# Decoder block on one core: output product from rounded parts, new order of TensorE's work in the sharing cycles, weight rests on POOL, last block's first products moved into attention

## The chip, the cores and the metric

One core of a Trainium2 chip runs the whole program. The engines are TensorE (PE in the profile, with its weight loads as PEld), VectorE (DVE), ScalarE (ACT), GpSimd (POOL) and SyncE (SP, which issues most of the DMAs). The metric is the device time in microseconds.

## The reference

```python
x = _layernorm(x + attn(x, up_w, gate_w, local_point, local_approx_output, fuse_weight, ...))   # 6 Taylor orders + SwiGLU, F = 1248
x = _layernorm(x + xattn(x, ctx, mask, position_bias, ln_weight, w_q, w_k, w_v, w_out))         # 32 heads of 128, 8 x 128 tokens
x = _layernorm(x + ffn(x, Wg, Wu, Wd, ag, au, ad))                                               # F = 1376, ternary weights

def xattn(h, kv, mask, bias, ln_weight, w_q, w_k, w_v, w_out):      # cut
    x = rmsnorm(h, ln_weight)
    q, k, v = heads(x @ w_q.T), heads(kv @ w_k.T), heads(kv @ w_v.T)
    score = einsum('bqhd,bkhd->bhqk', q, k) + bias
    score = softmax(where(mask, score, -inf));  score = where(mask, score, 0)
    return h + einsum('bhqk,bkhd->bqhd', score, v).reshape(...) @ w_out.T
```

All arrays are float32; x is 8 x 128 x 512. In these inputs the mask leaves at most the last 32 of 128 keys of each sample open, and the kernel has a path ("few") for that case.

## The kernel before

The eight samples are two halves of four (512 columns each). The first block runs for half 0 and half 1 (0 to about 221 us of the profile), cross attention from there to about 613, and the last feed-forward block to the end. float32 products that run in one pass use operands that are rounded on ACT ("hi", an fp32r copy) with the rest on DVE ("lo" = whole - hi, line 1288); hi·hi + hi·lo + lo·hi then makes three matmuls (`passes`, line 543). A plain float32 matmul stands in the profile as two weight loads and two MATMUL records.

Attention is 64 cycles n = 0..63, one per head and half, in four blocks of 16. In blocks 0 and 2 (n = 0..15 and 32..47) the cycle is a *sharing* one: it makes keys and values from rounded parts for both halves and keeps the other half's (`kept_k`, `kept_v`). In blocks 1 and 3 it is a *reading* one, with the kept ones. The names used below:

- `queries(n)` (line 716): 4 matmuls into bank 0, copied by ACT to `t_ring` (1160). Cycle n makes those of n+6.
- `keys(n)` (543, weights `wk_hi`, `wk_lo`): 12 matmuls into bank 1, copied by ACT. Cycle n makes those of n+7, so keys are made in cycles 0..8 and 25..40. `split_k` on ACT (1060) and `rest_k` on DVE (1288) prepare the weights.
- `values(n)` (543, weights in `b_hi`, `b_lo` by `split_v` on ACT, 1069, and `rest_v` on DVE): 12 matmuls into bank 3, copied to `v_sb` (1186).
- `turn(n)` (778): transposes the probabilities into bank 3, which ACT copies to `prob_t` (1167). The same bank holds the values.
- `outer(n)` (824): values times `wo` into bank 1, copied to `u_sb` (1193).
- `weigh(n)` (846): four matmuls of 32 rows each, one for each sample, probabilities times `u_sb`, added up in four accumulators. They use four different row groups of TensorE and run side by side.
- `group_scores` (729 and 751): in the second and third cycle of every four, the scores of the next four heads; `add_mask`, `find_max`, `divide` on DVE (1544, 1550 and 1552, 1558 to 1562) and `exponentials` on ACT (1174) make the softmax.
- `features` and `chunk`: transposes of the normalised rows and their copies, for the queries' second half (part 1) and for the last block (part 2, cycles 62 and 63).

The order is written out by hand for each engine as a loop over n, and every engine works strictly through its own list; semaphores tie them together. In cycle n TensorE's order before is queries(n+6), turn(n-1), weigh(n-2), keys(n+7), values(n), outer(n-1), scores. POOL does the normalisations' scales and rows (lines 445 to 485), two reductions over partitions (499, 509) and nothing in the cycles themselves. After the cycles come the last block's first `gate` and `up` (543, `A30`), and then a branch into the last block. ACT's silu of that first gate needs another table of functions (ACT_TABLE_LOAD).

## Time and profile before

| | us |
|---|---|
| median of 3 runs | 754.17 (753.99 to 755.84) |
| the profiled execution | 753.72 |
| its span | 751.9 |
| DVE busy | 522.2 (69%) |
| ACT busy | 408.6 (54%) |
| POOL busy | 94.8 (13%) |

The span runs from the first instruction to the last; 1.8 us of the execution lie around it. Busy times are sums over an engine's records, and shares are of the span. Matmul records overlap their neighbours, so the distance between the starts of two pieces of work is the better measure of what TensorE spends on one. PEclk is the granted share of TensorE's clock. "Idle" in brackets behind a row is the time in which the engine stood still ahead of it, with what released it ("issue": nothing that the profile shows).

### The profile page before, as it was taken

To read this page: it belongs to the slowest core of one execution; us is meant where nothing else is said; L and a number is where in the kernel's file an instruction comes from. 1 tells how busy PE (TensorE), PEld (TensorE's weight loads), DVE (VectorE), ACT (ScalarE), POOL (GpSimd) and SP (SyncE) were. 2 spreads that over 40 slices of the span, in tenths; PEclk is the share of its full clock that TensorE was granted. 3 is DMA by queue.
4 is the path that set the end of the run, shared out by engine and by line. 5 is a ranking of instruction groups with operands and counts; after the bars stand their busy time and mean duration, and the time that the engine had idled before them with its cause. 6 is when DMAs were issued, how large, how long until landed. Compare 5 with 4: busy or idle time off the path is not lost.

```text
span 751.9 us, 12237 instructions
## 1 busy us (share of the span) xinstructions
PE 716.2 (95%) x4082; PEld 555.7 (74%) x4082; DVE 522.2 (69%) x848; ACT 408.6 (54%) x747; POOL 94.8 (13%) x88
## 2 busy tenths in 40 slices
PE   8999999999999999999999999999999779998993
PEld 6788888888878878776667787877656257886882
DVE  6555687588664875686876678667897828669565
ACT  6333323432355676776776666666676644454552
POOL 2000000074003600000000000000050004105403
PEclk9999999999999999999999999999999999999997
DMA  8455532545556765677997776668785513442631
GB/s 307 152 206 206 179 119 70 163 168 187 183 208 199 251 195 181 216 258 233 306 316 236 240 238 190 192 215 267 263 297 180 169 44 117 135 151 98 204 122 56
DMA packets 70681, 145.10 MB, mean 193 GB/s; under 512 B 7920, under 2 KB 8192, under 8 KB 69984
## 3 DMA queue, kind: packets, MB, share of 16 engines
q1 hardware_dynamic: 69200, 137.26, 55.7%
q0 software_dynamic: 1200, 6.70, 2.3%
q8 instruction: 34, 0.56, 0.3%
q10 hardware_dynamic: 224, 0.39, 0.2%
q14 instruction: 23, 0.19, 0.1%
HBM read 142.23 MB, written 2.10 MB: 192 GB/s over the span
## 4 chain that ended last, share of the span: by engine, by line
PE 86%; DVE 5%; issue 3%; DMA 2%; ACT 2%; POOL 1%; SPq 0%; ACTq 0%; DVEq 0%; POOLq 0%
PE bank L543 38%; PE acc L543 16%; PE acc L846 8%; PE bank L751 7%; PE bank L824 7%; PE bank L716 7%; PE bank L778 1%; PE bank L729 1%; DMA b_raw<-b 1%; DMA a_raw<-a 1%; PE bank L575 1%; DVE tile_lo L1288 1%; ACT v_sb L1186 1%; DVE a_lo L1288 1%; DMA wq<-wqn 1%
## 5 line engine op out<-in xcount | busy, mean ns | idle before, releaser
L543 PE MATMUL bank<-feat_hi,a_hi 128*128 128x512 f32 x348 | 137.7, 396 | 2.2 <-ACT u_sb L1193 0.8
L543 PE MATMUL bank<-feat_lo,a_hi 128*128 128x512 f32 x348 | 136.5, 392 | 2.1 <-issue 2.1
L1288 DVE TENSOR_TENSOR a_lo<-a_raw,a_hi 128x1024 fp32r<-128x1024 f32 (+3 forms) x47 | 56.8, 1208 | 94.5 <-ACT a_hi L1000 86.9
L543 PE MATMUL acc<-b_hi,tile_hi 128*128 128x512 f32 x224 | 87.8, 392 | 4.9 <-DVE tile_lo L1288 3.0
L543 PE MATMUL acc<-b_hi,tile_lo 128*128 128x512 f32 x224 | 87.3, 390 | 0.0
L543 PEld LDWEIGHTS bank<-feat_hi,a_hi 128*128 128x128 f32 x348 | 65.9, 189 | 22.6 <-issue 4.0
L543 PEld LDWEIGHTS bank<-feat_lo,a_hi 128*128 128x128 f32 x348 | 65.9, 189 | 13.5
L846 PE MATMUL acc<-u_sb,prob_t 32*128 32x512 f32 x512 | 73.0, 640 | 0.0
L543 PE MATMUL bank<-feat_hi,a_lo 128*128 128x512 f32 x180 | 70.1, 389 | 0.0
L1017 ACT ACTIVATE tile_hi<-pair 128x512 fp32r<-128x512 f32 x54 | 33.9, 628 | 66.3 <-DVE pair L1350 37.4
L751 PEld LDWEIGHTS bank<-t_ring,xn 128*128 128x128 f32 x512 | 62.1, 192 | 8.5 <-issue 7.2
L445 POOL TENSOR_SCALAR scale<-moments 128x4 f32<-128x4 f32 (+1 forms) x9 | 2.6, 287 | 515.1 <-DVEq L1420 514.8
L1558 DVE TENSOR_REDUCE row_sum<-prob 128x4 f32<-128x512 f32 x64 | 43.7, 683 | 31.9 <-ACT prob L1174 30.5
L1160 ACT ACTIVATE t_ring<-bank 128x512 f32<-128x512 f32 x64 | 38.2, 597 | 46.3 <-PE bank L716 46.0
L751 PE MATMUL bank<-t_ring,xn 128*128 128x128 f32 x512 | 62.3, 275 | 0.0
L1193 ACT ACTIVATE u_sb<-bank 128x512 f32<-128x512 f32 x64 | 38.2, 598 | 28.4 <-PE bank L824 25.8
L543 PEld LDWEIGHTS acc<-b_hi,tile_hi 128*128 128x128 f32 x224 | 42.0, 188 | 15.6 <-DVE b_lo L1288 4.2
L543 PE MATMUL acc<-b_lo,tile_hi 128*128 128x512 f32 x136 | 52.9, 389 | 0.0
L1288 DVE TENSOR_TENSOR b_lo<-b_raw,b_hi 128x512 fp32r<-128x512 f32 x56 | 40.0, 715 | 14.9 <-ACT b_hi L1007 14.6
L1007 ACT ACTIVATE b_hi<-b_raw 128x512 fp32r<-128x512 f32 x56 | 34.8, 623 | 26.8 <-PE acc L543 21.6
L1026 ACT ACTIVATE gated<-bank 128x512 f32<-128x512 f32 x20 | 12.0, 598 | 67.8 <-PE bank L543 67.8
L543 PEld LDWEIGHTS acc<-b_hi,tile_lo 128*128 128x128 f32 x224 | 42.1, 188 | 8.6
(152 smaller groups left out, 1555.8 us busy)
## 6 DMA issues: line engine op xcount, KB each, us to landing
wqi<-ax SPq DMA_DIRECT2D x64, 256.0 KB, 3.3
wq<-wqn SPq DMA_DIRECT2D x64, 256.0 KB, 3.7
wv<-wvh SPq DMA_DIRECT2D x64, 256.0 KB, 4.0
wo<-bx SPq DMA_DIRECT2D x64, 256.0 KB, 4.0
a_raw<-w SPq DMA_DIRECT2D x22, 512.0 KB, 4.1
wk<-ax SPq DMA_DIRECT2D x43, 256.0 KB, 3.8
a_raw<-a SPq DMA_DIRECT2D x21, 512.0 KB, 5.4
b_raw<-b SPq DMA_DIRECT2D x34, 256.0 KB, 2.7
```

Source lines behind the costliest of these rows:

```text
L543: mm = pe.matmul(out_ap, w, x, start=start and k == 0, stop=stop and k == len(products) - 1, skip_group_check=True)
L716: mm = pe.matmul(bank[0][:, c * P:(c + 1) * P], wq[par][:, c * P:(c + 1) * P], few_keys, start=True, stop=True)
L751: mm = pe.matmul(bank[2][:, b * P:(b + 1) * P].rearrange("p (k h) -> p h k", h=GH), xn[half][:, c, b * SEQ:(b + 1) * SEQ], t_ring[g % 2][: ...
L824: mm = pe.matmul(bank[1][:], few_values, wo[slot][:], start=True, stop=True)
L846: mm = pe.matmul(acc[b][:], prob_t[par][rows, 0:P], u_sb[par][rows, :], start=begins, stop=ends, skip_group_check=True)
L1007: act.activation(b_hi[par][:], b_raw[par][:], ACT.Copy).then_inc(b_hi_ok, 1)
L1017: act.activation(tile_hi[par][:], src, ACT.Copy).then_inc(tile_hi_ok, 1)
L1026: act.activation(gated[:], bank[0][:], ACT.Silu).then_inc(silu_ok, 1)
L1160: act.activation(t_ring[n // GH % 2][:, n % GH].rearrange("p c b k -> p (c b k)"), bank[0][:], ACT.Copy).then_inc(t_ok, 1)
L1193: act.activation(u_sb[n % 2][:], bank[1][:], ACT.Copy).then_inc(u_ok, 1)
L1288: return dve.tensor_tensor(out_ap, whole, high, ALU.subtract)
L1558: dve.tensor_reduce(row_sum[:], prob[n % 2][:], AX_X, ALU.add).then_inc(sum_ok, 1)
```

## The change

Four things are changed in the attention path and one at its end.

1. In sharing cycles the output product of `weigh` is made of rounded parts: ACT writes `u_hi` in place of `u_sb` and also `p_hi` (128x128) from `prob_t`, DVE writes `p_lo` and `u_lo` (the latter from bank 1 and `u_hi`), and TensorE does 12 matmuls of 32 rows in fp32r in place of 4 in float32. Whoever writes bank 1 next waits for `u_lo_ok` as well.
2. TensorE's order in a sharing cycle becomes keys(n+7) between the two halves of queries(n+6), then turn, outer, values.
3. The rests of the key and value weights go to POOL, from the weights of n = 9 (keys) and n = 2 (values) on; DVE keeps the first ones. POOL's new loop stands behind its second reduction over partitions.
4. In reading cycles `values` (there only a mark) stands ahead of `weigh`, and ACT copies the values ahead of `copy_outer`.
5. The four transposes for the last block move to cycles 54, 57, 58 and 59, its first gate to cycle 60 and its first up to cycle 61 (into bank 2), its silu on ACT to cycle 62, and the loads that they need are issued at n = 50 and n = 58. The features of the last block have tiles of their own (`last_hi`, `last_lo`).

```diff
@@ POOL
             pool.tensor_copy(low_flag[:], piece_all[:, 1:2]).then_inc(flag_ok, 1)
+            for n in range(POOL_V - 1, HN):
+                k = n + LEAD_K + 1
+                if k < HN and shared(k):
+                    pool.wait_ge(wk_hi_ok, shared_count(k))
+                    pool.tensor_tensor(wk_lo[k % 2], wk[k % WK_RING][:], wk_hi[k % 2].bitcast(F32),
+                                       ALU.subtract).then_inc(wk_rest_ok, 1)
+                if n + 1 < HN and shared(n + 1):
+                    pool.wait_ge(wv_hi_ok, shared_count(n + 1))
+                    pool.tensor_tensor(wv_lo[(n + 1) % 2], wv[(n + 1) % 2][:], wv_hi[(n + 1) % 2].bitcast(F32),
+                                       ALU.subtract).then_inc(wv_rest_ok, 1)
             normalise(2)
@@ TensorE, keys
-                        pe.wait_ge(wk_lo_ok, shared_count(n))
+                        if n < POOL_K:                     # POOL_K = LEAD_K + 2 = 9
+                            pe.wait_ge(wk_lo_ok, n + 1)
+                        else:
+                            pe.wait_ge(wk_rest_ok, shared_count(n) - POOL_K)
@@ TensorE, weigh
+                    if few and shared(n):
+                        for k, (weights, values_) in enumerate(((p_hi, u_hi), (p_hi, u_lo), (p_lo, u_hi))):
+                            for b in range(HB):
...
+                                mm = pe.matmul(acc[b][:], weights[par][rows, :], values_[par][rows, :], start=begins and k == 0,
+                                               stop=ends and k == 2, skip_group_check=True)
@@ TensorE, the cycles
+                    if making:
                         keys(n + LEAD_K)
+                        if n >= 2:
+                            weigh(n - 2)
+                        if few:
+                            queries(n + LEAD_T, range(C // 2, C))
+                        if n >= 1:
+                            turn(n - 1)
+                            outer(n - 1)
...
+                        values(n)
...
                     if late:
+                        if n + LEAD_K < HN:
+                            keys(n + LEAD_K)
+                        turn(n - 1)
+                        if few:
+                            values(n)
+                        weigh(n - 2)
+                        if n in FEATURES_2:                # 54, 57, 58, 59
+                            features(2, FEATURES_2[n], resid[:, TT:2 * TT, :], min(n + LEAD_T + 1, HN))
...
                         outer(n - 1)
...
+                    if n == GATE_30:                       # 60
+                        pe.wait_ge(feat_lo_ok, C)
+                        gate(A30, A30 % 2, 0, HALVES * F1, last=True)
+                    if few and n == UP_30:                 # 61
+                        pe.wait_ge(added_ok, HN)
+                        up(A30 % 2, 0, HALVES * F1, last=True, into=bank[2])
@@ ACT
                 act.activation(prob_t[n % 2][:], bank[3][:], ACT.Copy).then_inc(turned_ok, 1)
+                if shared(n):
+                    act.wait_ge(turned_ok, n + 1)
+                    act.activation(p_hi[n % 2][:], prob_t[n % 2][:, 0:P], ACT.Copy).then_inc(p_hi_ok, 1)
...
+                if n == HN - 2:
+                    silu(A30, HALVES * F1, True, 0)
@@ DVE
+            def rest_p(n):
+                dve.wait_ge(p_hi_ok, shared_count(n))
+                low(p_lo[n % 2][:], prob_t[n % 2][:, 0:P], p_hi[n % 2][:].bitcast(F32)).then_inc(p_lo_ok, 1)
+            def rest_u(n):
+                dve.wait_ge(u_ok, n + 1)
+                low(u_lo[n % 2][:], bank[1][:], u_hi[n % 2][:].bitcast(F32)).then_inc(u_lo_ok, 1)
...
-                elif n > 0 and n + LEAD_K + 1 < HN and shared(n + LEAD_K + 1):
-                    rest_k(n + LEAD_K + 1)
+                if n >= 1 and shared(n - 1):
+                    rest_p(n - 1)
+                    rest_u(n - 1)
+                if 0 <= m < POOL_V:
+                    rest_v(m)
```

On TensorE, in a sharing cycle with keys, the program before stands like this (x4 are the four samples or the four chunks; `a_hi` are the keys' source features, `wk` the keys' weights, `b_hi` the values' weights):

```order
1985 L716 MATMUL bank<-k_ring,wq 128x128 x4
1986 L778 MATMUL bank<-ident_r,prob 128x128
1987 L846 MATMUL acc<-u_sb,prob_t 128x512 x4
1988 L543 MATMUL bank<-a_hi,wk_hi 128x256
...
2000 L543 MATMUL bank<-a_hi,b_hi 128x256
...
2012 L824 MATMUL bank<-wo,v_sb 128x512
```

The same cycle in the changed program:

```order
1669 L760 MATMUL bank<-k_ring,wq 128x128 x2
1670 L581 MATMUL bank<-a_hi,wk_hi 128x256
...
1682 L901 MATMUL acc<-u_hi,p_hi 128x512 x4
1683 L901 MATMUL acc<-u_lo,p_hi 128x512 x4
1684 L901 MATMUL acc<-u_hi,p_lo 128x512 x4
1685 L760 MATMUL bank<-k_ring,wq 128x128 x2
1686 L823 MATMUL bank<-ident_r,prob 128x128
1687 L874 MATMUL bank<-wo,v_sb 128x512
1688 L581 MATMUL bank<-a_hi,b_hi 128x256
```

The product and the keys have moved ahead of the turn (823), and only the outer product (874) stands between the turn and the values, which use the same bank 3.

On POOL, around its second reduction over partitions, the program before (ISA is an instruction that has no tile; here it changes the library of POOL's functions):

```order
40 L509 ISA
41 L509 ISA piece_all<-piece_all 128x1
42 L511 CAST low_flag<-piece_all 128x1
43 L445 ISA
44 L445 TENSOR_SCALAR scale<-moments 128x4
```

The changed program at the same place:

```order
42 L536 ISA piece_all<-piece_all 128x1
43 L538 CAST low_flag<-piece_all 128x1
44 L544 ISA
45 L544 TENSOR_TENSOR wk_lo1<-wk0,wk_hi1 128x512
46 L548 TENSOR_TENSOR b_lo0<-wv0,b_hi0 128x512
```

53 such subtractions now stand between the reduction and the normalisation of part 2 (23 for keys, 30 for values), and the first of them, the key weights of n = 9, directly behind the change of library.

## Rows read from the trace of the kernel before

**Rows 1.** The page, busy time: engine, busy us, share, instructions.
```profile
PE 716.2 (95%) x4082; PEld 555.7 (74%) x4082; DVE 522.2 (69%) x848; ACT 408.6 (54%) x747; POOL 94.8 (13%) x88
```
**Rows 2.** Windows: stretch, us; busy (instructions) by engine; PEclk, DMA share, GB/s.
```profile
430.54:533.81 103.27, 102.54 (x740) 80.01 (x741) 72.34 (x122) 69.49 (x146) 0.00 (x0) 1.00 0.68 221
533.81:573.88 40.07, 38.08 (x240) 24.05 (x240) 36.46 (x66) 28.78 (x56) 9.59 (x6) 1.00 0.82 276
573.88:613.11 39.23, 32.27 (x170) 16.80 (x171) 26.18 (x46) 22.99 (x40) 0.00 (x0) 1.00 0.34 114
```
**Rows 3.** Timeline, TensorE, sharing cycle 4: start, us, engine, line, operation, count.
```profile
272.65 1.05 PE L716 MATMUL bank<-k_ring,wq 128*128 128x128 f32 x8
273.54 0.28 PE L778 MATMUL bank<-ident_r,prob 128*128 128x128 f32 x1
273.75 1.14 PE L846 MATMUL acc<-u_sb,prob_t 32*128 32x512 f32 x8
274.82 0.38 PE L543 MATMUL bank<-a_hi,wk_hi 128*128 128x256 f32 x1
...
277.79 1.02 PE L824 MATMUL bank<-wo,v_sb 128*128 128x512 f32 x2
278.65 0.61 PE L716 MATMUL bank<-k_ring,wq 128*128 128x128 f32 x4
```
**Rows 4.** Timeline, TensorE and ACT, cycle 15, from turn to values.
```profile
345.66 0.28 PE L778 MATMUL bank<-ident_r,prob 128*128 128x128 f32 x1
...
346.36 0.59 ACT L1167 ACTIVATE prob_t<-bank 128x512 f32<-128x512 f32 x1
...
347.05 0.36 PE L543 MATMUL bank<-a_hi,b_hi 128*128 128x256 f32 x1
```
**Rows 5.** Timeline, DVE's rest of key weights 9; cycle 2 on TensorE.
```profile
256.89 0.68 DVE L1288 TENSOR_TENSOR wk_lo<-wk,wk_hi 128x512 fp32r<-128x512 f32 x1
...
258.87 1.06 PE L716 MATMUL bank<-k_ring,wq 128*128 128x128 f32 x8
...
261.05 0.39 PE L543 MATMUL bank<-a_hi,wk_hi 128*128 128x256 f32 x1
```
**Rows 6.** Timeline, POOL at its library changes, and the DVE reduction it awaits.
```profile
1.45 0.29 POOL L429 TENSOR_SCALAR_AFFINE_SELECT score<-score 128x128 f32<-128x128 f32 x1 [0.36 <-issue]
...
57.06 0.16 DVE L1502 TENSOR_REDUCE many<-many 128x1 f32<-128x8 f32 x1
...
60.20 0.38 POOL L499 PARTITION_ALL_REDUCE many<-many  x1 [11.23 <-issue]
...
263.12 0.38 POOL L509 PARTITION_ALL_REDUCE piece_all<-piece_all  x1 [6.03 <-issue]
263.56 0.19 POOL L511 CAST low_flag<-piece_all 128x1 int32<-128x1 f32 x1
```
**Rows 7.** Groups of instructions, POOL: busy us, mean ns, idle before.
```profile
L518 POOL TENSOR_TENSOR resid<-normed,resid 128x512 f32<-128x512 f32 x7 | 10.1, 1473 | 75.0 <-DVE normed L1401 38.7 <-DVE normed L1654 36.3
```
**Rows 8.** Timeline, POOL and DVE side by side after the last block's first half.
```profile
680.49 5.91 POOL L518 TENSOR_TENSOR resid<-normed,resid 128x512 f32<-128x512 f32 x4 [38.68 <-DVE normed L1401]
682.12 1.47 DVE L1288 TENSOR_TENSOR b_lo<-b_raw,b_hi 128x512 fp32r<-128x512 f32 x1
```
**Rows 9.** Windows, over the stretch of low clock, columns as in rows 2.
```profile
616.60:620.00 3.40, 3.40 (x10) 2.57 (x9) 0.23 (x1) 1.90 (x3) 0.00 (x0) 0.52 0.01 4
```
**Rows 10.** Timeline, TensorE, a short reading cycle, queries to turn.
```profile
366.95 1.05 PE L716 MATMUL bank<-b_raw,wq 128*128 128x128 f32 x8
368.33 0.36 PE L778 MATMUL bank<-ident_r,prob 128*128 128x128 f32 x1 [0.33 <-ACT v_sb L1186]
```
**Rows 11.** The chain that ended last, gate with up, later one up: start, us.
```profile
39.19 5.44 PE bank L543 x24
...
608.38 3.01 PE bank L543 x12
```
**Rows 12.** Timeline, ACT, table load ahead of the last block's first silu.
```profile
602.85 1.28 ACT L1024 ACT_TABLE_LOAD   x1
```

More of the change, by code:

```diff
@@ L127, in sem @@
             return ctx.enter_context(nc.semaphore(name))
+        with ExitStack() as sharing:
+            u_lo = [sharing.enter_context(nc.sbuf_tensor(f"u_lo{i}", [P, D], F32R)) for i in range(2)]
         a_raw, a_hi, a_lo = two("a_raw", [P, 2 * C * P]), two("a_hi", [P, 2, C, P], F32R), two("a_lo", [P, 2, C, P], F32R)
@@ L154, in decoder_kernel @@
         wk.append(gated)
+        with ExitStack() as sharing:
+            u_hi = [sharing.enter_context(nc.sbuf_tensor(f"u_hi{i}", [P, D], F32R)) for i in range(2)]
         u_sb = two("u_sb", [P, D])
@@ L177, in decoder_kernel @@
         piece = [raw.bitcast(I32) for raw in piece_raw]
+        with ExitStack() as sharing:
+            p_hi = [sharing.enter_context(nc.sbuf_tensor(f"p_hi{i}", [P, P], F32R)) for i in range(2)]
         mask_words = sb("mask_words", [P, BATCH, SEQ // 4], U32)
@@ L180, in decoder_kernel @@
         mask_add = [sb(f"mask_add{j}", [P, BATCH, P], BF16) for j in range(GH)]
+        with ExitStack() as sharing:
+            p_lo = [sharing.enter_context(nc.sbuf_tensor(f"p_lo{i}", [P, P], F32R)) for i in range(2)]
         few_add, key_scale = sb("few_add", [P, BATCH, FEW]), sb("key_scale", [P, 2])
@@ L545, in passes, with project @@
                 return mm
-            def project(bank_, par, which, half, x_hi=feat_hi, x_lo=feat_lo, low=True):
+            def project(bank_, par, which, half, low=True, last=False):
+                x_hi, x_lo = (last_hi, last_lo) if last else (feat_hi, feat_lo)
                 for c in range(C):
@@ L713, in queries @@
                         few_keys = kept_k[n % BLOCK]
[L714 removed]
+                    for c in chunks:
                         if few:
@@ L866, in attention @@
                     g, j = n // GH, n % GH
+                    making = 0 <= n < HN and shared(n)
+                    late = 0 <= n < HN and not shared(n)
                     if n < 0:
@@ L875, in attention @@
                             pe.wait_ge(xn_ok, 2 * C)
-                        queries(n + LEAD_T)
-                    late = 0 <= n < HN and not shared(n)
-                    if late and n + LEAD_K < HN:
-                        keys(n + LEAD_K)
-                    if n == HN:
-                        weigh(n - 2)
-                        pe.wait_ge(feat_lo_ok, C)
-                        gate(A30, A30 % 2, 0, HALVES * F1)
-                    if n >= 1:
-                        turn(n - 1)
-                    if 2 <= n < HN:
-                        weigh(n - 2)
+                        if n - 1 in FEATURES_2:
+                            pe.wait_ge(feat_lo_ok, FEATURES_2[n - 1] + 1)
+                        queries(n + LEAD_T, range(C // 2) if few and making else range(C))
+                    if n == -LEAD_K:
+                        down(T30 - 1, (T30 - 1) % 2, 1, last=True)
                     if not few and 0 <= n < HN and j < 2:
@@ L913, in attention @@
                         head_scores(n + 1)
+                if not few:
+                    pe.wait_ge(added_ok, HN)
+                    up(A30 % 2, 0, HALVES * F1, last=True, into=bank[2])
                 pe.wait_ge(u_ok, HN)
-                up(A30 % 2, 0, HALVES * F1)
                 weigh(HN - 1)
@@ L954, in last_block @@
                 transposes(3, 1, bank[3], x1)
-                gate(a, a % 2, 0, s0 + f, low=low)
+                gate(a, a % 2, 0, s0 + f, low=low, last=True)
                 pe.wait_ge(feat_lo_ok, C + 1)
@@ L1192, in copy_outer @@
                     act.wait_ge(out_used, n - 1)
[L1193 removed]
+                act.activation(u_hi[n % 2][:] if shared(n) else u_sb[n % 2][:], bank[1][:], ACT.Copy).then_inc(u_ok, 1)
             for n in range(-LEAD_K, HN):
[L1196 to L1199 removed]
+                making, late = n >= 0 and shared(n), n >= 0 and not shared(n)
@@ L1341, in few_bias_rests, with product @@
                         few_bias_hi[:, part * GH:(part + 1) * GH, :].bitcast(F32)).then_inc(few_bias_ok, 1)
-            def product(a, done, m, mpar, last_block, f):
+            def product(a, done, m, mpar, last_block, f, second=bank[1]):
                 dve.wait_ge(silu_ok, done + 1)
@@ L1616, in _ @@
             split_a(A30 + 1, (A30 + 1) % 2)
-            product(A30, s0, T30, T30 % 2, True, 0)
+            product(A30, s0, T30, T30 % 2, True, 0, second=bank[2])
             split_b(T30, T30 % 2)
```

213 lines of the change are left out of this document (125 added, 88 removed).

## Prediction

> **What bounds the kernel now.** I read the page's busy times first: TensorE is busy 95% of the span [rows 1]. Then the windows by stage [rows 2]: in sharing block 2 (430.54 to 533.81) it is busy 102.5 of 103.3 us, while DVE has 72.3 and ACT 69.5, so only what TensorE does or waits for counts there. In reading block 3 up to 573.88 DVE is at 36.5 of 40.1, close to a bound beside TensorE's 38.1. From there to the last block TensorE is busy 32.3 of 39.2: waits set the time.
>
> Inside a sharing cycle the timeline gives TensorE's prices by distances of starts [rows 3]: queries 273.54 - 272.65 = 0.89, turn 0.21, weigh 1.07, keys and values together 2.97 (1.485 each), outer 0.86; the cycle is 6.00 long, and 0.89 + 0.21 + 1.07 + 2.97 + 0.86 is 6.00. No gap. Cycles without keys have 1.485 less, those with scores about 1.8 or 2.2 more, unchanged here.
>
> **POOL's first rest: a new wait.** This is the largest term. Keys(9) are issued in cycle 2. Before, their weights' rest was ready on DVE at 256.89 + 0.68 = 257.57, and the keys began at 261.05 [rows 5]. In the new order they stand behind half of queries(8): 258.87 + 0.89 / 2 = 259.3, and they now need POOL's first subtraction. POOL works through its list in order and reaches it only behind the second reduction over partitions, whose cast ends at 263.56 + 0.19 = 263.75 [rows 6]. So TensorE stands still at least until then, with weigh(0), turn, outer and values queued behind the keys in its own list; nothing on another engine can take up that time.
>
> Behind the cast comes the change of library back, x. It is bounded by two rows. Below: at the start POOL's first such change left 0.36 us of idle time. Above: the change ahead of the second reduction left 6.03 us [rows 6]. The first reduction shows how 6.03 may be made up: what it waited for, DVE's 57.06 + 0.16 = 57.22, was 2.98 before its start at 60.20, although the change of library had been issued some 11 us before. So about 3.0 belongs to the first call of the reduction, and 6.03 - 2.98 = 3.05 to the change itself. A subtraction is an ordinary function, not one brought in by the library, so I take x = 3.05. The subtraction itself takes 1.47, as POOL's other TENSOR_TENSOR of this shape [rows 7], plus 0.1 for the signal. The keys start at 263.75 + 3.05 + 1.47 + 0.1 = 268.4, and 268.4 - 259.4 gives +8.9 (with x at its ends, +6.2 and +11.9; I shift the start by 0.1 for the stalls of cycle 1). The later rests are in time: the next two are done 3 us later, values(2) stand 4 us behind the keys, keys(10) 6 us, and two rests a cycle cost POOL 2.9 of 6 us.
>
> The GPSIMD Engine Reference of the Trainium skill (section Instruction dispatch) says that the first call of a freshly loaded kernel pays about 6 us in which no instruction is shown. The trace agrees for the reduction (6.03). If the rule held for the first subtraction too, x would be 6.03, the stall 11.9 and the time about 3 us above the forecast; that is the second case below.
>
> **Clock after that wait.** The trace shows the granted clock at 0.52 over 616.6 to 620.0 [rows 9], after TensorE had been idle for about half of the 5.6 us before: the lower level, and 3.4 x 0.48 = 1.6 us lost. A wait of 9 us is longer than any pause in the attention of before. I add +2.5: once this event and half of it again (between 0 and 3.5).
>
> **The product from rounded parts.** weigh before is 1.07: four float32 products of 32 rows side by side take little more than outer, one product of the same 512 columns (0.86), so 0.21 goes into changing over [rows 3]. 12 one-pass matmuls are three rounds of four. A one-pass matmul of 256 columns costs 2.97 / 24 = 0.124 us, one of 512 columns 5.44 / 24 = 0.227 [rows 11]. If the four of a round run side by side: 3 x 0.227 + 0.21 = 0.89, a gain of 0.18 a cycle. Bounds: 0.70 (0.64 and nearly nothing for changing over), and 12 x 0.227 = 2.72 if they do not overlap. I take 0.89, since the overlap of row groups is what rows 3 show.
>
> **The new order.** values(n) need bank 3 copied after turn(n-1). In cycle 15 one sees that path bare: turn 345.66, ACT's copy 346.36 to 346.95 (behind the copy of the queries), values 347.05, so 1.39 from turn to values [rows 4]. Before, weigh and keys lay between and hid it (2.55). Now only turn and outer do, 0.21 + 0.86 = 1.07: a wait of 0.32 in each sharing cycle. With keys: 6.00 - 0.18 + 0.32 = 6.14, +0.14 in 17 cycles = +2.4. Without keys the cycle of before had part of this wait already (1.39 against 0.21 + 1.07, so 0.11): 0.32 - 0.18 - 0.11 = +0.03 in 14 = +0.4. Together +2.8. Cycle 8, with two of the copies of features around its values, I charge +0.5.
>
> **ACT and DVE.** ACT gets 32 copies of 128x128, some 0.3 each; ACT was busy 69.5 of 103.3, so they are hidden. DVE loses 53 rests of 0.69 (36.6) and gets 32 of 0.69 and 32 small ones of 0.3 (31.7). The new wait on u_lo, ahead of keys(n+8): outer ends, ACT's copy 0.6, DVE 0.69, against values 1.49 plus half the queries 0.45 and the 0.3 of wait; some 0.3 us of slack, which costs nothing as long as DVE is free.
>
> DVE is not quite free. While POOL runs its TENSOR_TENSOR, DVE's subtraction of two SBUF tiles takes 1.47 [rows 8] in place of 0.68 [rows 5]. A sharing cycle has two such steps of softmax (lines 1552 and 1562), and POOL is at work for up to 2.9 of its 6.1 us. Stretched, DVE's cycle grows from about 4.5 by at most 1.6 to 6.1: just the cycle. I take +0.5 in all (0 to +9).
>
> The same reference (section Specifications) says that GpSimd and VectorE share their SBUF interfaces when a Vector instruction has two SBUF inputs, which is a rule against this change; the trace agrees, 1.47 against 0.68.
>
> **Reading cycles.** The short ones (no keys, no scores) have 1.38 between queries and turn, of which 0.89 is work: TensorE waits for v_sb, which ACT copies behind u_sb [rows 10]. With the values copied first the 0.49 goes. Four such cycles in block 1: -2.0, and -0.4 for smaller waits of the same kind in the others. In block 3 DVE is at 36.5 of 40.1 [rows 2], so I take -1.5 of the possible 3.
>
> **The end.** Up, 3.01 of the chain [rows 11], and the gate ahead of it, as much again, leave the stretch behind cycle 63, and so do the transposes from cycles 62 and 63, for cycles 54 to 61. After cycle 58 a cycle has only turn, weigh and outer, about 2.2 us of TensorE work, and the stretch had 6.9 us idle [rows 2], so part fits in and part lengthens it: cycles 60 and 61 become 5.1 to 5.8. And the silu with its table load, 1.28 [rows 12] + 0.69, now stands on ACT ahead of the copies that weigh(62) needs: a wait of 1.9 there, and 0.9 twice more where outer's copy is awaited. Laid out by hand from the turn at 573.88 I come to 35.4 in place of 39.2: -3.8 (between -6 and 0). The stall and the low clock at the start of the last block stay.
>
> **Sum.** 8.9 + 2.5 + 2.8 + 0.5 + 0.5 - 2.4 - 1.5 - 3.8 = +7.5. On the profiled execution's 753.72 (its span of 751.9 and 1.8 around it, which stays) that is 761.2; the median of the runs was 0.45 higher, so 761.7.
>
> **The cases.**
> - *Forecast*, 761.7: chance 0.36; with its own unknowns 757 to 766.
> - *The first subtraction pays the whole 6.03*: +3, 764.7; for it, the only row of a change of library in mid-program that is followed at once; against it, the 2.98 of the first reduction. 0.20.
> - *DVE and POOL in each other's way*: if every rest stretches a step of softmax, DVE's cycle of 6.1 is above TensorE's in the cycles where masks are added twice, and u_lo comes late: 0.5 in 17 cycles, +8.5, 770. It decides from about 1.6 us of stretching a cycle on. 0.16.
> - *The rounded matmuls do not run side by side*: 2.72 - 0.89 = 1.83 in 31 cycles, 818. Against it: rows 3. 0.04.
> - *Gains and the wait cancel*: the library's change costs 0.36 (-2.7) and the clock one event only (-0.8), and the end gives 5.5 in place of 3.8: 756.5, just within 0.3% of before. 0.12.
> - *Faster*: the same short wait, and weigh at 0.70 (-0.19 x 31 = -5.9): 752.3; with reading block 3 (-1.5) and the end (-2.2) at their better bounds 748.6, which is the number for this case. It decides from a weigh of about 0.75 on. For it: TensorE is the bound of these cycles and every tenth of weigh counts 3 us. 0.12.
>
> 0.3% is 2.3 us, about what a measurement of this kernel can tell from no change. Faster 0.12, within it 0.12, slower 0.76. The range of 8 in 10 leaves out the better half of the last case, the 818 and the worst of DVE's: 751 to 771.
>
> **What would show it.** In the changed profile: TensorE idle from about 259.4 to 268.4, released by POOL, or the term is wrong; the granted clock at one half after it; weigh to the next queries 0.89; turn to values 1.39 in the sharing cycles and the cycles with keys at 6.14; DVE's steps of softmax at 0.69 or above; no wait for v_sb in reading cycles; 35.4 from the turn of cycle 57 to the last block. A first POOL rest before 260 would make the prediction wrong as a whole.

## The result and the profile after

| | us |
|---|---|
| before, median of 4 runs | 754.58 (753.99 to 755.84) |
| changed, median of 4 runs | 778.69 (777.21 to 779.26) |
| ratio | 1.0314, 95% interval 1.0294 to 1.0335 |
| span of the profiled executions | 751.9 before, 775.4 changed |

Slower, as forecast, but by 24.1 us where 7.5 were forecast, and outside the range of 751 to 771. One execution of all that follow was slow, 3981 us in the old order's run; that kernel's median of 757.00 is 756.50 without it. The page's busy times of the changed kernel, against [rows 1]:

```profile
PE 719.2 (93%) x4210; PEld 563.5 (73%) x4210; DVE 531.2 (69%) x859; ACT 417.4 (54%) x779; POOL 164.5 (21%) x141
```

TensorE has 3.0 us more work in a span 23.5 us longer: it waits. The windows say where. They are cut at the same turns in both kernels, those of cycles 1, 16, 31, 48 and 57 (columns as in [rows 2]). The third begins at cycle 31 and not 32, because cycle 32's keys stand behind its turn before and ahead of it in the changed kernel. Before:

```profile
252.40:350.60 98.20, 97.48 (x705) 76.72 (x706) 68.14 (x115) 66.93 (x139) 5.26 (x5) 1.00 0.67 216
350.60:426.90 76.30, 74.75 (x505) 52.93 (x506) 58.81 (x103) 52.73 (x105) 0.00 (x0) 1.00 0.83 276
426.90:533.80 106.90, 105.85 (x761) 81.79 (x760) 75.00 (x126) 72.43 (x152) 0.00 (x0) 1.00 0.69 222
533.80:573.90 40.10, 38.10 (x240) 24.08 (x240) 36.48 (x66) 28.81 (x56) 9.59 (x6) 1.00 0.82 276
573.90:751.90 178.00, 154.07 (x698) 114.89 (x698) 116.55 (x174) 85.09 (x130) 36.72 (x31) 0.97 0.38 123
```

Changed:

```profile
253.20:369.80 116.60, 98.52 (x752) 78.29 (x750) 70.72 (x121) 68.97 (x152) 31.40 (x26) 0.94 0.53 177
369.80:447.60 77.80, 74.78 (x513) 53.72 (x514) 58.36 (x100) 53.43 (x106) 9.43 (x7) 1.00 0.83 274
447.60:559.40 111.80, 107.62 (x818) 83.37 (x816) 78.71 (x130) 76.23 (x167) 32.69 (x25) 1.00 0.62 206
559.40:600.60 41.20, 37.77 (x251) 25.27 (x252) 38.10 (x70) 30.14 (x58) 9.59 (x6) 1.00 0.83 283
600.60:775.40 174.80, 152.88 (x696) 115.86 (x694) 116.64 (x174) 84.55 (x129) 36.94 (x31) 0.96 0.39 126
```

The four stages up to the turn of cycle 57 all grew, the reading ones too. Only the last window, with the end of attention and the last block, shrank. The first sharing block alone has 18.4 of the 23.5. That block's wait stands in the timeline of TensorE and POOL:

```profile
258.55 0.61 PE L760 MATMUL bank<-k_ring,wq 128*128 128x128 f32 x4
...
263.62 0.38 POOL L536 PARTITION_ALL_REDUCE piece_all<-piece_all  x1 [6.62 <-issue]
264.06 0.19 POOL L538 CAST low_flag<-piece_all 128x1 int32<-128x1 f32 x1
271.85 1.25 POOL L544 TENSOR_TENSOR wk_lo<-wk,wk_hi 128x512 fp32r<-128x512 f32 x1 [7.61 <-issue]
...
273.31 0.55 PE L581 MATMUL bank<-a_hi,wk_hi 128*128 128x256 f32 x1 [14.15 <-issue]
```

It is the forecast chain in the forecast place: half of queries(8), the reduction, the cast, idle time, the first subtraction, keys(9). The idle time behind the cast is 7.61 and not 3.05. The granted clock, by windows over the wait and behind it:

```profile
266.00:270.00 4.00, 0.00 (x0) 0.00 (x0) 0.00 (x0) 0.00 (x0) 0.00 (x0) 0.50 0.00 0
...
275.00:276.00 1.00, 1.00 (x6) 0.92 (x5) 0.00 (x0) 0.00 (x0) 0.58 (x1) 0.50 0.00 0
276.00:277.00 1.00, 1.00 (x13) 0.66 (x12) 0.00 (x0) 0.75 (x2) 0.00 (x0) 0.73 0.05 16
277.00:278.00 1.00, 1.00 (x14) 0.79 (x7) 0.00 (x0) 0.06 (x2) 0.00 (x0) 1.00 0.00 0
```

It fell to one half, the lower of its two levels, while TensorE stood still, and was whole again some 3.2 us after work resumed: 1.6 lost by the clock. By the starts, keys(9) to the next turn took 4.45 (273.31 to 277.76) for work of 3.06 at the full clock, so 1.4.

A sharing cycle with keys is now 6.32 in place of 6.00. TensorE's timeline of cycle 36, against [rows 3]:

```profile
486.74 0.61 PE L760 MATMUL bank<-k_ring,wq 128*128 128x128 f32 x4
487.10 0.36 PE L581 MATMUL bank<-a_hi,wk_hi 128*128 128x256 f32 x1
...
488.70 0.51 PE L901 MATMUL acc<-u_hi,p_hi 32*128 32x512 f32 x4
489.04 0.40 PE L901 MATMUL acc<-u_lo,p_hi 32*128 32x512 f32 x4
489.27 0.41 PE L901 MATMUL acc<-u_hi,p_lo 32*128 32x512 f32 x4
489.61 0.71 PE L760 MATMUL bank<-k_ring,wq 128*128 128x128 f32 x4
490.16 0.28 PE L823 MATMUL bank<-ident_r,prob 128*128 128x128 f32 x1
490.28 1.02 PE L874 MATMUL bank<-wo,v_sb 128*128 128x512 f32 x2
491.54 0.36 PE L581 MATMUL bank<-a_hi,b_hi 128*128 128x256 f32 x1 [0.24 <-issue]
```

Half the queries 0.36, keys 1.60, weigh 0.91, the other half 0.55, turn to values 1.38, and the values 1.52 (485.22 to 486.74 in the cycle before): 6.32. Without keys a cycle went from 4.64 to 4.87, though the forecast gave it only 0.03: there the two halves of the queries stand on both sides of weigh and take 0.54 and 0.55 (345.19 to 345.73 and 346.63 to 347.18), 1.09 for the 0.89 in one piece.

In reading block 3 the short cycles are 3.13 in place of 3.63 to 3.71, but the distance from the turn of cycle 52 to that of cycle 53 grew from 3.86 to 5.25. Timeline of the changed kernel:

```profile
579.47 0.63 ACT L1265 ACTIVATE prob<-score 128x512 f32<-128x512 f32 x1 [1.74 <-DVE score L1668]
580.89 1.10 PE L874 MATMUL bank<-wo,kept_v 128*128 128x512 f32 x2 [1.72 <-issue]
583.07 0.39 PE L823 MATMUL bank<-ident_r,prob 128*128 128x128 f32 x1 [0.19 <-DVE prob L1678]
```

ACT stands still for DVE's step on the scores, its copies come behind that, and the next turn waits for DVE's division. DVE itself works there almost without a gap: from one division to the fourth after it, its list (softmax, masks, residual, statistics) takes 19.75 before (534.90 to 554.65) and 21.20 changed (561.13 to 582.33). The 1.45 more are `p_lo` and `u_lo` with a gap of 0.55 between them. So up to the turn of cycle 53 this stage goes at DVE's pace in both kernels.

### The profile page after: what moved, and what is told of

Its sections match the earlier page's. It is cut to its first block, busy times and chain, and to the rows that moved or that the text cites. A ratio compares the mean times of both kernels' runs of the same rounds, so it can differ in the third digit from the quotient of the medians.

```text
span 775.4 us, 12751 instructions
## 1 busy us (share of the span) xinstructions
PE 719.2 (93%) x4210; PEld 563.5 (73%) x4210; DVE 531.2 (69%) x859; ACT 417.4 (54%) x779; POOL 164.5 (21%) x141
## 4 chain that ended last, share of the span: by engine, by line
PE 81%; issue 6%; DVE 4%; ACT 4%; DMA 3%; POOL 1%; SPq 1%; ACTq 0%; DVEq 0%; POOLq 0%
PE bank L581 36%; PE acc L581 16%; PE bank L796 7%; PE bank L760 7%; PE bank L874 6%; PE acc L912 3%; PE acc L901 3%; PE bank L774 1%; DMA b_raw<-b 1%; PE bank L823 1%; DMA a_raw<-a 1%; PE bank L614 1%; DMA wq<-wqn 1%; DMA wv<-wvh 1%; POOL resid L556 1%
## 5 line engine op out<-in xcount | busy, mean ns | idle before, releaser
L581 PE MATMUL bank<-feat_hi,a_hi 128*128 128x512 f32 x260 | 102.4, 394 | 0.4 <-DVE a_lo L1394 0.4
L581 PE MATMUL bank<-feat_lo,a_hi 128*128 128x512 f32 x260 | 101.7, 391 | 0.0
L581 PE MATMUL bank<-feat_hi,a_lo 128*128 128x512 f32 x172 | 67.0, 389 | 0.0
L548 POOL TENSOR_TENSOR b_lo<-wv,b_hi 128x512 fp32r<-128x512 f32 x30 | 38.4, 1281 | 122.5 <-ACT b_hi L1157 122.5
L581 PEld LDWEIGHTS bank<-feat_hi,a_hi 128*128 128x128 f32 x260 | 49.2, 189 | 11.9 <-DVE a_lo L1394 1.6
L581 PEld LDWEIGHTS bank<-feat_lo,a_hi 128*128 128x128 f32 x260 | 49.3, 189 | 10.1
L581 PE MATMUL bank<-a_hi,wk_hi 128*128 128x256 f32 x128 | 39.2, 306 | 17.4 <-issue 15.8
L1678 DVE TENSOR_TENSOR prob<-prob,row_inv 128x512 f32<-128x512 f32 x64 | 52.0, 812 | 2.2
L1668 DVE TENSOR_TENSOR score<-score,neg_max 128x512 f32<-128x512 f32 x64 | 50.4, 788 | 2.2
```

The costliest lines, as they stand in the source:

```text
L548: pool.tensor_tensor(wv_lo[(n + 1) % 2], wv[(n + 1) % 2][:], wv_hi[(n + 1) % 2].bitcast(F32), ALU.subtract).then_inc(wv_rest_ok, 1)
L581: mm = pe.matmul(out_ap, w, x, start=start and k == 0, stop=stop and k == len(products) - 1, skip_group_check=True)
L1668: dve.tensor_tensor(score[n % GH][:], score[n % GH][:], neg_max[:].unsqueeze(2).broadcast_to([P, HB, SEQ]), ALU.add).then_inc(shifted_ok, 1)
L1678: dve.tensor_tensor(prob[n % 2][:], prob[n % 2][:], row_inv[:].unsqueeze(2).broadcast_to([P, HB, SEQ]), ALU.mult).then_inc(prob_ok, 1)
```

## The experiments

All are timed beside the kernel before (medians of 754.4 to 755.0; 1.8 of each time lies around the span). The cycle lengths are distances between the starts of successive turns, and a length is named after the cycle in which the second turn stands. In three groups: the wait on POOL, the sharing cycle, the hand-over to reading cycles with the end.

**Reduction moved.** The two instructions go behind POOL's list:

```diff
-            pool.partition_all_reduce(piece_all[:, 1:2], piece_all[:, 0:1], P, ...)   # and the cast
             for n in range(POOL_V - 1, HN):
...
+            pool.partition_all_reduce(piece_all[:, 1:2], piece_all[:, 0:1], P, ...)   # and the cast
             normalise(2)
```

> The changed kernel, with POOL's second reduction over partitions and its cast moved behind POOL's list of rests (their result is first read after the attention). Theory: TensorE's 14.15 us of idle time in cycle 2 and the half clock of about 3.2 us behind it (1.6 lost) come from POOL's first subtraction standing behind the reduction, the cast and 7.61 of idle time; with them gone 778.7 - 15.8 = 763, and TensorE's gap between the halves of queries(8) and keys(9) under 1 us. Rival 1, the 7.61 belongs to the first subtraction itself (a first use), not to what stands ahead of it: a stall of about 7.6 + 1.3 - 2 = 7 us stays, 770. Rival 2, the stall only moves: with it gone transfers or DVE are late somewhere else in the first block, 767 or more. By both the sharing cycle with keys stays at 6.32.

763.10 (ratio to before 1.0119, 1.0097 to 1.0142): 15.6 less than the changed kernel, with 15.8 in the theory. POOL's first subtraction now begins as soon as the rows are normalised, and the keys do not wait for it; timeline:

```profile
256.57 1.56 POOL L512 TENSOR_SCALAR normed<-resid,rms_scale 128x512 f32<-128x512 f32 x1
...
258.11 1.28 POOL L539 TENSOR_TENSOR wk_lo<-wk,wk_hi 128x512 fp32r<-128x512 f32 x1
...
260.05 0.36 PE L580 MATMUL bank<-a_hi,wk_hi 128*128 128x256 f32 x1
```

No idle time ahead of the first subtraction: the 7.61 belong to what stood ahead of it. Cycles with keys stay at 6.32. Without the wait the kernel is still 8.7 slower than before (763.10 against 754.36).

**Probe on POOL**, in the kernel before, where nothing waits for POOL:

```diff
             pool.tensor_copy(low_flag[:], piece_all[:, 1:2]).then_inc(flag_ok, 1)
+            pool.tensor_scalar(probe[:, 0:1], exponent[:, 0:1], 2.0, None, ALU.mult).then_inc(probe_ok, 1)
+            pool.wait_ge(probe_ok, 1)
+            pool.tensor_tensor(probe[:, 1:2], probe[:, 0:1], exponent[:, 0:1], ALU.subtract).then_inc(probe_ok, 1)
```

> The kernel before, with two small POOL instructions (a TENSOR_SCALAR and a TENSOR_TENSOR of 128x1) directly behind the second cast, where POOL has nothing to do for 284 us: their time can hide. Theory: any first ordinary instruction behind a reduction pays the change of library, so the TENSOR_SCALAR starts 7 to 8 us behind the cast and the TENSOR_TENSOR right behind it. Rival 1: only a subtraction pays (the TENSOR_SCALAR starts at once, the TENSOR_TENSOR 7 us later). Rival 2: neither pays, and the 7.61 were a wait for something else (weights or their rounded part). Time as before, 754 to 755, by all.

754.21 in its one execution, and POOL's timeline:

```profile
263.86 0.38 POOL L511 PARTITION_ALL_REDUCE piece_all<-piece_all  x1 [6.79 <-issue]
264.31 0.51 POOL L513 CAST low_flag<-piece_all 128x1 int32<-128x1 f32 x1
272.06 0.59 POOL L514 TENSOR_SCALAR probe<-exponent 128x1 f32<-128x1 f32 x1 [7.25 <-issue]
272.73 0.19 POOL L516 TENSOR_TENSOR probe<-probe,exponent 128x1 f32<-128x1 f32 x1
```

The first instruction behind the reduction and its cast pays some 7 us, be it this TENSOR_SCALAR of 128x1 or the changed kernel's subtraction of 128x512, and the next one pays nothing. The kernel before has the same change of library there and 284 us for it, so its trace cannot show the price.

**All rests on DVE**, in the changed kernel:

```diff
-POOL_K, POOL_V = LEAD_K + 2, 2
+POOL_K, POOL_V = HN, HN
...
+                elif n > 0 and n + LEAD_K + 1 < HN and shared(n + LEAD_K + 1):
+                    rest_k(n + LEAD_K + 1)
...
-                if 0 <= m < POOL_V:
+                if 0 <= m < HN and shared(m):
                     rest_v(m)
```

> The changed kernel with all rests of weights back on DVE, POOL's list of rests empty; order and product as changed. Theory A (DVE had room, the division brought nothing but the stall): the stall goes, and 763 as with the reduction moved. Theory B (DVE needs the relief, since the rests of probabilities and of outer's product now come on top): DVE's work in a cycle with keys is 3.6 of softmax + 0.28 + 4 x 0.69 less one, 5.9 to 6.0 of 6.32 before any gap between steps, so u_lo comes late: 0.2 to 0.5 in 17 cycles, 767 to 771. Rival C (POOL's work slows DVE by more than it relieves it): under 761.

759.81 (1.0085, 1.0055 to 1.0114). Rival C has the number, but not the reason. DVE has room for everything (sharing cycles are 6.32 here too), and the kernel is 3.3 faster than with the reduction moved. By turns, cycles 25, 28, 29 and 32 are 0.54, 0.33, 0.34 and 0.34 shorter: the ones ahead of and at the start of the next sharing block in which keys are made, where a rest of 1.27 on POOL is late and one of 0.69 on DVE is not. That is 1.55; the profiles differ by 0.95 more before the first turn and as much in the last block, which the edit doesn't touch. That last difference of 1.9 in sum is not explained. POOL did slow DVE, as the groups show (busy, mean ns). Changed kernel:

```profile
L1678 DVE TENSOR_TENSOR prob<-prob,row_inv 128x512 f32<-128x512 f32 x64 | 52.0, 812 | 2.2
L1668 DVE TENSOR_TENSOR score<-score,neg_max 128x512 f32<-128x512 f32 x64 | 50.4, 788 | 2.2
L1660 DVE TENSOR_TENSOR score<-bank,mask_add 128x512 f32<-128x512 f32 x64 | 42.3, 682 | 1.4 <-PE bank L796 1.4
```

Rests on DVE:

```profile
L1668 DVE TENSOR_TENSOR score<-score,neg_max 128x512 f32<-128x512 f32 x64 | 44.3, 693 | 2.2
L1678 DVE TENSOR_TENSOR prob<-prob,row_inv 128x512 f32<-128x512 f32 x64 | 44.3, 692 | 2.2
L1660 DVE TENSOR_TENSOR score<-bank,mask_add 128x512 f32<-128x512 f32 x64 | 42.4, 683 | 1.4 <-PE bank L796 1.4
```

The two steps that read SBUF alone were stretched by 13.8 us in sum, the one that reads a bank by none; DVE's slack took it all.

**weigh behind turn**, with the reduction moved:

```diff
                         keys(n + LEAD_K)
-                        if n >= 2:
-                            weigh(n - 2)
                         if few:
                             queries(n + LEAD_T, range(C // 2, C))
                         if n >= 1:
                             turn(n - 1)
+                            if n >= 2:
+                                weigh(n - 2)
                             outer(n - 1)
```

> The kernel with the reduction moved, and besides weigh(n-2) put between turn(n-1) and outer(n-1) in the sharing cycles, where it stood ahead of the second half of the queries. Theory: turn to values is 1.38 bare, and only 0.12 + 0.86 of work cover it, so 0.40 a cycle is waiting; with weigh's 0.9 between them it is covered: a cycle with keys 5.92 in place of 6.32, 31 cycles, 12 us less than the reduction moved alone, 751. Rival 1, keys(n+7) and outer then wait for the rest of outer's product, which has less time: cycle 6.1 to 6.3, 757 to 763. Rival 2, the 0.4 is a price of changing between kinds of matmul and not a wait: it stays, 763.

750.72 (0.9949, 0.9926 to 0.9972): faster than before. A cycle with keys is 5.82. TensorE's timeline:

```profile
465.15 0.61 PE L759 MATMUL bank<-k_ring,wq 128*128 128x128 f32 x4
465.59 0.28 PE L822 MATMUL bank<-ident_r,prob 128*128 128x128 f32 x1
465.80 0.50 PE L900 MATMUL acc<-u_hi,p_hi 32*128 32x512 f32 x4
...
466.70 1.12 PE L873 MATMUL bank<-wo,v_sb 128*128 128x512 f32 x2
467.26 0.69 PE L580 MATMUL bank<-a_hi,b_hi 128*128 128x256 f32 x1
```

Of the 0.50, some 0.31 is the wait from turn to values (1.38 less the 0.21 and 0.86 of turn and outer); the rest was lost in changing over, as keys behind which queries follow take 1.52 (1.60 with weigh behind them), and the second half of the queries 0.44 (0.55).

**The same with the rests on DVE** (both edits above):

> weigh(n-2) between turn(n-1) and outer(n-1), and all rests of weights on DVE. With the rests on DVE and the old place of weigh, the four reading cycles in which keys are made took 0.54, 0.33, 0.34 and 0.34 less than with them on POOL (a rest of 0.69 against 1.27, with the keys waiting for it), 1.55 together, and no other cycle differed. Theory: the same 1.6 goes here, 750.7 - 1.6 = 749.1. Rival: at 5.82 a cycle DVE (5.9 of work and gaps) is now the bound with all rests on it: 0.1 to 0.4 in 17 cycles, 752 to 757.

749.20 (0.9923, 0.9902 to 0.9945); sharing cycles 5.82, so DVE is not the bound. The 1.5 is as expected and about what these runs can tell.

**float32 product** in the kernel with weigh behind turn (no `p_hi`, `p_lo`, `u_lo`, four matmuls):

```diff
-                    if few and shared(n):
-                        for k, (weights, values_) in enumerate(((p_hi, u_hi), (p_hi, u_lo), (p_lo, u_hi))):
...
-                act.activation(u_hi[n % 2][:] if shared(n) else u_sb[n % 2][:], bank[1][:], ACT.Copy)
+                act.activation(u_sb[n % 2][:], bank[1][:], ACT.Copy)
```

> The kernel with weigh behind turn and the reduction moved, with the product back in float32: four matmuls from the copied probabilities and outer's copy, no rounded parts and no rests of them. Theory: the rounded product is worth what TensorE's row shows, 1.07 against 0.90, 0.17 in 32 cycles = 5.4; the rests of outer's product made two reading cycles wait about 0.6 each, which goes: 750.7 + 5.4 - 1.2 = 755; a cycle with keys 5.99. Rival 1, the rests and copies for the rounded product cost more than that on ACT and DVE: 750 or less. Rival 2, changing between kinds of matmul costs less around the rounded product than around the float32 one: above 757.

750.47, no different from 750.72 of the kernel with weigh behind turn. The parts are there: cycles with keys 5.99 against 5.82, so 0.17 each in favour of the rounded product. But cycles 17 and 49 take 3.21 here against 4.32, and 19 and 51 4.92 against 5.66 and 5.62: the rounded product gives back 3.7 where a sharing block ends. By these parts 1.6 should be left of its 5.3, and the profiled spans are 1.3 apart (749.2 and 747.9), but the medians don't show it. The changed kernel's timeline shows both waits:

```profile
374.11 0.36 PE L823 MATMUL bank<-ident_r,prob 128*128 128x128 f32 x1 [1.02 <-DVE u_lo L1394]
...
377.68 2.72 DVE L1513 SCALAR_TENSOR_TENSOR resid<-acc,row_valid,resid 128x512 f32<-128x512 f32 x4
...
379.70 1.87 PE L912 MATMUL acc<-u_sb,prob_t 32*128 32x512 f32 x8
```

In cycle 17 turn stands behind keys(24), which issue nothing but wait for the last `u_lo`; in cycle 18 weigh(16) takes 1.80 to the next start where 1.07 is its price. It begins a new sum and needs DVE to have read the old one from the accumulators, which ends at 380.4, late by DVE's rests.

**Old order with the rounded product** (queries, turn, weigh, keys, values, outer on TensorE, ACT and DVE likewise; rests on DVE):

```diff
-                        queries(n + LEAD_T, range(C // 2) if few and making else range(C))
+                        queries(n + LEAD_T, range(C))
...
                     if making:
-                        keys(n + LEAD_K)
+                        if n >= 1:
+                            turn(n - 1)
                         if n >= 2:
                             weigh(n - 2)
-                        if few:
-                            queries(n + LEAD_T, range(C // 2, C))
-                        if n >= 1:
-                            turn(n - 1)
-                            outer(n - 1)
...
+                        keys(n + LEAD_K)
                         values(n)
...
+                        if n >= 1:
+                            outer(n - 1)
```

> The product from rounded parts alone in the sharing cycles, in the order that TensorE, ACT and DVE had before (queries, turn, weigh, keys, values, outer), rests of weights on DVE; reading cycles and end as changed. Theory: weigh(n-2) now follows outer(n-2) by only 1.1 (queries and turn), while outer's copy 0.6, the rest 0.69 and their signals need 1.5 or more behind values' copy on ACT: a wait of 0.5 to 1 in 32 cycles, cycle 6.3 to 6.8: 765 to 780. Rival: rests and copies come in time and the cycle is 5.82 to 5.9: 749 to 751.

757.00 (1.0029, 1.0015 to 1.0042), below the 765 of the theory and above the 751 of the rival. Its wait is real but not in every cycle: of four cycles with keys two are as with weigh behind turn in the new order (7.61 and 5.82) and two longer (6.46 for 5.82 and 8.71 for 8.06). Timeline of one that waits:

```profile
466.53 0.69 DVE L1394 TENSOR_TENSOR u_lo<-bank,u_hi 128x512 fp32r<-128x512 f32 x1 [0.78 <-ACT u_hi L1283]
466.59 0.28 PE L823 MATMUL bank<-ident_r,prob 128*128 128x128 f32 x1
467.43 0.51 PE L901 MATMUL acc<-u_hi,p_hi 32*128 32x512 f32 x4 [0.56 <-issue]
```

The rest of outer's product is ready at 467.22 and weigh begins at 467.43. With the rounded product the new order, with weigh behind turn, is worth some 7.5 (749.20 against 757.00); with weigh ahead of turn, as changed, it was some 3 slower than the old order (759.81).

**Values' copy in its old place**, behind outer's, in reading cycles:

```diff
-                    copy_values(n)
                     if n in FEATURES_2:
                         chunk(2, FEATURES_2[n], bank[0])
                     copy_outer(n - 1)
+                    copy_values(n)
```

> The kernel with weigh behind turn and the rests on DVE, with ACT in reading cycles copying outer's product first and the values behind it, as the kernel before did. Theory: the values' place is worth 0.49 in each of the short reading cycles (3.14 against 3.63), and the cycles with keys lose nothing by it now that the rests are on DVE: seven short cycles up to cycle 56 give +3.4, 752.5. Rival: weigh and the keys waited for outer's copy (0.67 and 0.84 in the changed kernel) and gain what the short cycles lose: 749 to 750.

753.49 (0.9982, 0.9966 to 0.9997), 4.3 above the same kernel without the edit. Short cycles are 3.63 and 3.71 again instead of 3.13. Cycle 22 goes the other way, 5.47 against 6.51: behind two short cycles at 3.13 TensorE waits there instead, for the transfer of `wv`, by the profile (0.67 in the changed kernel, 1.06 in the same kernel without the edit).

**TensorE's wait handed to ACT**:

```diff
-                    if n > LEAD_K + 1:
-                        pe.wait_ge(u_lo_ok, shared_count(n - LEAD_K - 2))
                     if few and not shared(n):
                         pe.sem_inc(k_mm, 1)
                         return
+                    if n > LEAD_K + 1:
+                        pe.wait_ge(u_lo_ok, shared_count(n - LEAD_K - 2))
...
+                if n > LEAD_K + 1 and not shared(n):
+                    act.wait_ge(u_lo_ok, shared_count(n - LEAD_K - 2))
```

> The kernel with weigh behind turn and the rests on DVE, where the keys of a reading head (which issue nothing) do not make TensorE wait for the rest of outer's product any more; ACT waits for it ahead of its copy. Theory: in cycles 17 and 49 turn stood 1.0 behind that wait (4.32 against 3.71 before); with it gone 0.6 each, 1.2 together, 749.1 - 1.2 = 748. Rival: ACT then stands still in TensorE's place and turn's copy is as late as before: no difference, 749.

748.65 against 749.20, which these runs cannot tell apart. Cycle 17 fell from 4.32 to 3.13, and cycles 18 and 19 rose from 5.38 to 5.98 and from 5.65 to 6.24. Neither the theory nor the rival had this: the wait moved one cycle on.

**Last two heads of each sharing block in float32**, weigh behind turn, rests on DVE:

```diff
+def rounded(n):
+    return shared(n) and n % BLOCK < BLOCK - 2
...
-                    if few and shared(n):
+                    if few and rounded(n):
                         for k, (weights, values_) in enumerate(((p_hi, u_hi), (p_hi, u_lo), (p_lo, u_hi))):
```

> The kernel with weigh behind turn and the rests on DVE, where the last two heads of each sharing block (14, 15, 46, 47) keep the float32 product and so have no rounded parts. Theory: the rounded product is worth 0.17 in each sharing cycle (5.82 against 5.99), but its rests on DVE run into the reading block: cycles 17 and 19, and 49 and 51, were 1.1 and 0.74 longer with it than without (4.32 against 3.21, 5.65 against 4.92). Without rests of the last two heads this goes, 3.7, for 4 x 0.17 = 0.7 of lost gain: 749.2 - 3.0 = 746.2. Rival: DVE is late there for its other work (residual, masks) and the wait only moves to cycles 18 and 22, as when TensorE's wait was handed to ACT: 748.5 to 749.5.

745.42 (0.9870, 0.9854 to 0.9886), the fastest: 3.8 below the same kernel without the edit. Cycles 17 and 49 are 3.23 and 3.24, 19 and 51 4.92, cycles with keys 5.82, and 18 and 22 did not grow.

**silu one head later**, on top:

```diff
-                if n == HN - 2:
+                if n == HN - 1:
                     silu(A30, HALVES * F1, True, 0)
```

> As with the last two heads in float32, and ACT's silu of the last block with its table load one head later, behind outer's copy for weigh(62). Theory: in the end stretch TensorE waited 1.78 for that copy, and 0.67 and 0.78 more; they were made by the silu ahead of it. 1.8 goes there, and up to 1 of it comes back where weigh(63) waits for its copies behind the silu: 1 to 2 less than without the move, 745. Rival: the gate of the next step waits for the silu anyway, and what is won ahead of weigh(63) is lost behind it: within 0.5 of the kernel without the move.

746.48 against 745.42: nothing won, as the rival had it. The wait ahead of weigh(62) fell from 1.78 to 0.78, so 0.78 is not the silu's. The one ahead of weigh(63) grew from 0.78 to 1.18, and TensorE's idle time ahead of the last block's gate from 3.03 to 4.71.

**Queries in one piece** behind the keys, on top of the last two heads in float32:

```diff
-                        queries(n + LEAD_T, range(C // 2) if few and making else range(C))
+                        queries(n + LEAD_T) if not (few and making) else None
...
-                            queries(n + LEAD_T, range(C // 2, C))
+                            queries(n + LEAD_T)
```

> As with the last two heads in float32, with the queries in one piece behind the keys in the sharing cycles (not halves around them). Theory: the half ahead of the keys covers the time in which DVE makes the rest of outer's product: keys could start 0.16 to 0.2 before it is there, so keys wait 0.2 in 17 cycles, and nothing is won by joining: +3, 749. Rival: changing between kinds of matmul once less is worth 0.1 and more a cycle and the wait is shorter: 744 to 745.

750.51, 5.1 slower. The cycles with keys that have no scores around them are 6.24 in place of 5.82, and keys wait for DVE's rest, as the timeline shows:

```profile
464.11 0.69 DVE L1402 TENSOR_TENSOR u_lo<-bank,u_hi 128x512 fp32r<-128x512 f32 x1 [0.56 <-ACT u_hi L1292]
...
464.58 0.28 PE L589 MATMUL bank<-a_hi,b_lo 128*128 128x256 f32 x1
465.05 0.36 PE L589 MATMUL bank<-a_hi,wk_hi 128*128 128x256 f32 x1 [0.19 <-DVE u_lo L1402]
```

So the halves are what covers that rest.

## Why the prediction was right in kind and wrong in size

By profiled spans, and with keys(8) allowed for (they stand ahead of turn(0) in the new order: 1.49), the 23.5 are:

| | forecast | measured |
|---|---|---|
| wait for POOL's first rest | +8.9 | +14.15 |
| clock behind it | +2.5 | +1.6 |
| sharing cycles with cycle 8 and DVE/POOL | +3.8 | +4.1 and +4.8 |
| reading blocks | -3.9 | +1.6 and +1.2 |
| end and last block | -3.8 | -3.2 |
| ahead of the first turn | 0 | -0.7 |

- **POOL's first rest.** The mechanism was right, and the reduction moved shows it: 15.6 of the 24 go. The step that failed is "6.03 - 2.98 = 3.05 to the change itself". I gave part of the idle time ahead of the reduction to its first call and the remainder to the change of library. Behind the reduction 7.61 and 7.25 stand idle, more than ahead of it (6.03 to 6.79 in these runs). That is 4.6 of the 5.3 that the wait was too long; 0.5 more is the cast, which ended at 264.25 and not 263.75. Nothing in the trace of before showed it, because POOL's next instruction came 284 us later: my ends were 0.36 and 6.03, and the value lay above both. The second case had 6.03 in its sum and was nearer, though it put the cost on the first subtraction; by the probe a TENSOR_SCALAR pays it too. The rule of the Trainium skill (GPSIMD Engine Reference, Instruction dispatch), about 6 us for the first call of a freshly loaded kernel, was the better guide; both runs are above its figure.
- **Sharing cycles.** weigh at 0.91 (0.89) and turn to values at 1.38 (1.39) are as forecast. What failed is "keys and values together 2.97": they cost that only in one piece. Apart, with other kinds of matmul around them, they are 1.60 and 1.52, so a cycle is 6.32 and not 6.14. This is 3.1 in 17 cycles; a part of the rest is the queries, which cost 1.09 and not 0.89 in cycles without keys.
- **DVE and POOL.** "Stretched", yes: 812 and 788 ns against 692 and 693; but no sharing cycle was longer for it: 6.32 with the rests on either engine. The case of 770 did not come.
- **Reading cycles.** "With the values copied first the 0.49 goes" held in each short cycle (3.13 to 3.14 against 3.63), and values' copy in its old place gives it back. What failed is that I costed the stage by that wait alone. Others took its place: the last `u_lo` ahead of turn in cycles 17 and 49 and the late sum behind it (3.7, by the float32 product and by the last two heads in float32), POOL's slower rests of keys (1.55 by the rests on DVE, of which the 0.34 of cycle 32 lies in the second sharing block), and `wv`'s transfer in cycle 22. In block 3 DVE's list, which the forecast had called close to a bound, was the bound: +2.1 up to the turn of cycle 53 and -0.9 behind it, with 0.5 of moved transposes in cycle 54, where I had taken -1.5. "Nothing as long as DVE is free" was said of `u_lo` inside the block and not asked of its end.
- **The end.** -3.2 for -3.8, in part by luck. From the turn of cycle 57 to the last block's next gate it is 37.5 (600.63 to 638.12), not 35.4, for 39.3 before (573.88 to 613.14). The other 1.5 was won behind that point, where nothing was forecast: before, TensorE stood still for 0.67 ahead of this gate and for 2.13 within it, and now for 3.44 ahead of it. The waits of 1.78 and 0.78 for outer's copy are there, but only 1.0 of the 1.78 is the silu's, and it is not a price to be saved: the silu one head later shows another wait behind it.

The sum of the misses: 5.3 for the wait less 0.9 of clock, 5.1 in the sharing cycles, 6.7 in the reading ones, 0.6 in the end, less 0.7 ahead of the first turn: 16.1, for 23.5 against 7.5. Without the wait and its clock the forecast came to -3.9 (7.5 - 11.4), so faster than before, and the measured rest is +7.8. The direction was right by the first term alone; for the rest together even the sign was wrong.

Open is why 7.3 to 7.6 us stand idle behind a reduction and 6.0 to 6.8 ahead of it. That the change of library is what takes them fits its place in the program, between the cast and the instruction that pays, but no run has the one without the other. How much of the first reduction's 11 us of idle time was the same is open too.

## What to carry to other kernels

Before handing an engine a second list of work, ask what its first instruction will stand behind, and take a cost that was always hidden as unknown upwards as well: here two instructions moved in the text were worth 15.6 us. A matmul's price holds for the run in which it was measured; one that is cut off from its own kind cost 0.04 to 0.2 more here, and an order should put other engines' round trips behind the longest piece that doesn't need them (weigh between turn and values: 12.4 us). And a wait saved in a stage is only the first of several: look at the hand-over to the next stage, where the engines that had slack in the middle are last.

## What the runs showed of the hardware

- POOL, behind a reduction over partitions: 7.61 and 7.25 us without a shown instruction ahead of the first one that is not its cast (a TENSOR_TENSOR, a TENSOR_SCALAR), and none ahead of the cast (0.1 behind the reduction) or of the next instruction.
- DVE beside a POOL subtraction: two-input steps from SBUF 692 to 812 ns on average, a step with one input from a bank 683 to 682 ns.
- TensorE: 12 one-pass matmuls of 32 rows in 0.90, their three rounds starting 0.34 and 0.23 apart, so four row groups side by side.
